# A recurrent kernel on one core: TensorE's program of the GRU stage written out, without a buffer for the current layer's weights

## The reference, cut to what matters

```python
A = (adj != 0).astype(x.dtype)
h = x
for l in range(weight.shape[0]):            # 5 layers
    m = jnp.einsum('bnd,de->bne', h, weight[l])
    agg = jnp.einsum('bij,bid->bjd', A, m)
    h = _gru_cell(agg, h, w_ih, w_hh, b_ih, b_hh)
return h * mask[..., None]
# _gru_cell: gi = agg @ w_ih.T + b_ih; gh = h @ w_hh.T + b_hh
#            r, z = sigmoid(i_r + h_r), sigmoid(i_z + h_z); n = tanh(i_n + r * h_n)
#            h = (1 - z) * n + z * h
```

## Time and profile before

| | |
|---|---|
| median of 3 runs | 584.0 us (583.87 to 584.15) |
| profiled execution, span from first to last instruction | 583.5 us |
| mean granted clock of TensorE over the span | 0.965 |
| TensorE busy | 533.1 us, 91% |
| VectorE busy | 464.4 us, 80% |
| ScalarE busy | 379.3 us, 65% |
| POOL busy | 225.2 us, 39% |
| the 20 copies to wcur, VectorE | 28.5 us |

### The profile page before, as it was taken

How to read it: one execution, slowest core, us unless ns; L and a number is a source line. 1 busy time by engine, 2 the same in 40 slices (tenths; PEclk the granted TensorE clock), 3 DMA queues, 4 the chain that set the end, 5 groups by cost and what they waited for, 6 DMA issues and landing times.

```text
span 583.5 us, 9958 instructions
## 1 busy us (share of the span) xinstructions
PE 533.1 (91%) x2955; PEld 445.0 (76%) x2955; DVE 464.4 (80%) x1000; ACT 379.3 (65%) x703; POOL 225.2 (39%) x278
## 2 busy tenths in 40 slices
PE   5877799999999999999999999999999999999980
PEld 3676689788888888787887887878878878788760
DVE  4416587698888889888888899788888997887884
ACT  3331456667677766687687766877777658667653
POOL 6644351224334242434443323434443333333434
PEclk9676999999999999999999999999999999999995
DMA  4646470000000000000000000000000000000002
GB/s 113 151 105 174 121 203 0 1 0 2 0 0 0 2 0 1 2 18 18 0 18 2 19 0 0 18 18 0 18 0 18 1 1 19 4 14 18 2 18 72
DMA packets 34930, 17.06 MB, mean 29 GB/s; under 512 B 4117, under 2 KB 34810, under 8 KB 34906
## 3 DMA queue, kind: packets, MB, share of 16 engines
q1 hardware_dynamic: 32170, 15.47, 9.9%
q0 software_dynamic: 1280, 0.58, 0.7%
q10 hardware_dynamic: 1456, 0.72, 0.4%
HBM read 12.54 MB, written 4.19 MB: 29 GB/s over the span
## 4 chain that ended last, share of the span: by engine, by line
PE 50%; DVE 16%; SPq 10%; issue 8%; ACT 7%; POOL 7%; DVEq 1%; DMA 0%; ACTq 0%; POOLq 0%
PE p L1036 12%; PE p L1038 12%; PE p L1037 12%; PE p L1029 7%; PE p L1023 5%; DVE wcur L827 5%; SPq L275 4%; SPq L281 3%; POOL rs L417 3%; DVE cg L879 2%; DVE cg L882 2%; ACT rg L605 2%; DVE dg L842 2%; POOL nm L415 2%; SPq L287 2%
## 5 line engine op out<-in xcount | busy, mean ns | idle before, releaser
L458 POOL TENSOR_TENSOR dg<-hT,ng 128x512 f32<-128x512 f32 x80 | 122.3, 1528 | 284.1 <-ACT ng L617 284.1
L1036 PE MATMUL p<-ghi,wcur 128*128 128x512 f32 x240 | 101.4, 422 | 7.6 <-DVE wcur L827 7.6
L1036 PE MATMUL p<-hhi,wh 128*128 128x512 f32 x240 | 101.4, 423 | 4.7 <-ACT zg L615 4.3
L1038 PE MATMUL p<-ghi,wcur 128*128 128x512 f32 x240 | 94.5, 394 | 0.0
L1038 PE MATMUL p<-hhi,wh 128*128 128x512 f32 x240 | 94.4, 393 | 0.0
L1037 PE MATMUL p<-hlo,wh 128*128 128x512 f32 x240 | 94.2, 393 | 0.0
L1037 PE MATMUL p<-glo,wcur 128*128 128x512 f32 x240 | 93.9, 391 | 0.0
L1029 PEld LDWEIGHTS p<-an,nat 128*128 128x128 f32 x640 | 83.4, 191 | 6.3
L879 DVE SCALAR_TENSOR_TENSOR cg<-p,biasc,rg 128x512 f32<-128x512 f32 x80 | 59.8, 748 | 34.6 <-ACT rg L605 34.6
L1029 PE MATMUL p<-an,nat 128*128 128x128 f32 (+1 forms) x640 | 84.2, 274 | 0.0
L605 ACT ACTIVATE rg<-p,gb 128x512 f32<-128x512 f32 x80 | 55.2, 690 | 44.5 <-PE p L1038 39.4
(11 more groups left out here) (125 smaller groups left out, 838.5 us busy)
## 6 DMA issues: line engine op xcount, KB each, us to landing
xn<-in_x_dram SPq DMA_DIRECT2D x8, 512.0 KB, 5.2
an<-in_adj_dram SPq DMA_DIRECT2D x8, 512.0 KB, 7.2
out_dram<-tile_data SPq DMA_DIRECT2D x16, 256.0 KB, 2.3
w<-in_L_gnn_W_dram SPq DMA_DIRECT2D x2, 640.0 KB, 5.2
tile_data<-in_x_dram SPq DMA_DIRECT2D x16, 50.0 KB
tile_data<-in_x_dram POOLq DMA_DIRECT2D x16, 24.0 KB, 2.6
zg<-in_L_gnn_weight_dram ACTq DMA_DIRECT2D x1, 320.0 KB, 3.6
tile_data<-in_x_dram SPq DMA_DIRECT2D x8, 36.0 KB
```

Source lines behind the costliest of these rows:

```text
L458: nc.gpsimd.tensor_tensor(dg[:, w.slot % 2, :], hT[:, w.slot, :], ng[:, w.slot % 2, :], ALU.subtract).then_inc(d_ok, 1)
L1036: MM(bank[:], w[:, 0, cols], xhi, start=start, stop=False)
L1038: return MM(bank[:], w[:, 1, cols], xhi, start=False, stop=stop)
```

## The change

`supergroup` and `windows` get a switch. With it, the layers 1 to 3 are a Python loop, so their windows are written out in the program text, and the layer number is a constant in each. TensorE alone takes the switch. VectorE, ScalarE and POOL keep the hardware loop over layers, and all keep the one over chunks. TensorE reads the fused weights straight from wf. The tile wcur, its semaphore, the 20 copies on VectorE with their waits for z_ps, and TensorE's 20 waits for them are removed.

```diff
-def supergroup(eng, sg, first=False, more=True):
+def supergroup(eng, sg, first=False, more=True, unrolled=False):
...
-    with eng.Fori(1, LAYERS - 1) as l:
-        for slot in range(SLOTS):
-            yield Window(sg, l, slot, "step", "step", **norms(l, slot))
+    if unrolled:
+        for l in range(1, LAYERS - 1):
+            for slot in range(SLOTS):
+                yield Window(sg, l, slot, "step", "step", **norms(l, slot))
+    else:
+        with eng.Fori(1, LAYERS - 1) as l:
+            for slot in range(SLOTS):
+                yield Window(sg, l, slot, "step", "step", **norms(l, slot))
...
-        wcur = sb("wcur", [128, 2, GATES], f32r)
...
-            def layer_weights(l):
-
-                nc.vector.tensor_copy(wcur[:], wf[:, bass.ds(l, 1)].rearrange("p o h e -> p (o h) e")).then_inc(wcur_ok, 1)
-
...
-            layer_weights(0)
...
-                    last_layer = isinstance(w.l, int) and w.l == LAYERS - 1
-                    if s == SLOTS - 1 and not (last_layer and not w.enter):
-
-                        wait_alone(dve, z_ps, k + 1)
-                        layer_weights(0 if last_layer else w.l + 1)
...
-            for w in windows(pe):
+            for w in windows(pe, unrolled=True):
...
-                    if s == 0:
-                        pe.wait_ge(wcur_ok, w.sg * LAYERS + w.l + 1)
...
-                    product(PR, wcur, 0, xhi, xlo, False, True).then_inc(r_ps, 1)
+                    wl_now = wf[:, w.l]
+                    product(PR, wl_now, 0, xhi, xlo, False, True).then_inc(r_ps, 1)
...
-                    product(PI, wcur, 2, xhi, xlo, True, True).then_inc(i_ps, 1)
-                    product(PZ, wcur, 1, xhi, xlo, False, True).then_inc(z_ps, 1)
+                    product(PI, wl_now, 2, xhi, xlo, True, True).then_inc(i_ps, 1)
+                    product(PZ, wl_now, 1, xhi, xlo, False, True).then_inc(z_ps, 1)
```

More of the change, by code:

```diff
@@ L131, in supergroup, with windows @@
                      enter=more and slot >= 2, **share)
-def windows(eng):
+def windows(eng, unrolled=False):
     yield opening(0, first=True)
-    yield from supergroup(eng, 0, first=True)
+    yield from supergroup(eng, 0, first=True, unrolled=unrolled)
     yield opening(1)
     with eng.Fori(1, CHUNKS - 1) as sg:
-        yield from supergroup(eng, sg)
+        yield from supergroup(eng, sg, unrolled=unrolled)
         yield opening(sg + 1)
-    yield from supergroup(eng, CHUNKS - 1, more=False)
+    yield from supergroup(eng, CHUNKS - 1, more=False, unrolled=unrolled)
     yield None
@@ L256, in build @@
         r_ok, z_ok, n_ok, t1_ok, c_ok, d_ok, e_ok, h_ok = map(sem, ("r_ok", "z_ok", "n_ok", "t1_ok", "c_ok", "d_ok", "e_ok", "h_ok"))
-        hi_ok, lo_ok, nat_ok, ghi_ok, glo_ok, wcur_ok = map(sem, (
-            "hi_ok", "lo_ok", "nat_ok", "ghi_ok", "glo_ok", "wcur_ok"))
+        hi_ok, lo_ok, nat_ok, ghi_ok, glo_ok = map(sem, ("hi_ok", "lo_ok", "nat_ok", "ghi_ok", "glo_ok"))
         bn1, ln1_st, ln1_rs, ln1_ok, x2_ok, sum_ok, bn2, ln2_st, ln2_rs, ln2_ok, out_ok = map(sem, (
```

## The result

| | before | after |
|---|---|---|
| median of the runs | 584.08 us (4 runs) | 564.13 us (563.64 to 565.27, 4 runs) |
| span of the profiled execution | 583.5 us | 563.6 us |
| first to last block of neighbour products | 438.50 us | 417.93 us |
| before the first of these blocks | 117.01 us | 117.63 us |
| behind the last | 28.0 us | 28.0 us |

The ratio is 0.9651, interval 0.963 to 0.9672. The forecast was 563.8 us. The profiled execution took 565.27 us, 1.67 above its span. Of the 19.9 us by which the span fell, the stage gave 20.57; the part before it was 0.6 us longer, the tail the same.

A forecast was written before the change was run, and what follows sets the result against it. TensorE was taken to bound the stage, with 22.2 us over its floor. Gains of 11.7 + 7.6 + 0.9 = 20.2 us took the 583.5 us span to 563.3, plus 0.5 gives 563.8 us; range 561.5 to 568.5.

The forecast's parts named there:

- The floor: Recurrent stage: a window with TensorE always busy takes 5.48 us, twelve with new samples 0.44 more; 416.3 us in all.
- Slot 0, 11.7 us: Slot 0 of layers 1 to 4: TensorE no longer waits for the wcur copy, gaining 0.73 us in 16 windows.
- Slot 1, 7.6 us: Slot 1, chunks after the first: without the copy, statistics and zg come earlier, gaining 0.63 us in 12 windows.
- The change of chunk, 0.9 us: Six windows around each chunk change: VectorE gets ahead without the copy; 0.3 us each time, bounds 0 and 2.8 us.
- How 0.48 us of idle time makes 0.73: TensorE after a stop: first product takes 0.50 us in place of 0.39 and its weight load is no longer covered.
- The two bills: The copy costs slot 0 by TensorE's wait, 11.7 us, and slot 1 by delaying statistics and zg, 7.6 us.
- The longer code at nothing: TensorE's code grows from 12 to 20 windows of text per chunk; claimed to cost nothing, covered by queued work.
- rivals 2 and 3: TensorE's longer code: chunk-loop jumps fetch again, 568.4 us, chance 0.06; or TensorE starves for code, 620 us, chance 0.03.
- Rival 2: TensorE's chunk loop: each of two jumps back over 20 windows fetches code, 4.6 us in all, 568.4 us; chance 0.06.
- Rival 1: Slot 1: TensorE's wait moves to zg and stays, so the 7.6 us are not gained, 571.4 us; chance 0.07.
- The port: VectorE and POOL share an SBUF port pair: sixteen copies took 1.64 us, four 0.54, long ones during POOL's subtraction.
- VectorE's busy time: VectorE loses 20 copies and twelve register operations; its busy time was to fall by some 28 us.

The follow-up runs named there:

- the last experiment: Changed kernel with ScalarE's copy of new samples to nat moved ahead of ghi around a chunk change: ratio 0.9603 to the kernel before, median 561.93 us.

## Why the prediction was right, point by point

- *The floor.* 5.48 us was right for every window inside a chunk. For windows with new samples I took 5.48 + 0.44 = 5.92 us, while the row has 5.94; the last experiment shows eight of the twelve at 5.88. The stage at its floor is thus 416.1 and not 416.3 us.
- *Slot 0, 11.7 us.* The sixteen windows fell from a mean of 6.22 to 5.48: 11.8 us.
- *Slot 1, 7.6 us.* Twelve windows fell from 6.11 to 5.48: 7.6 us. The mechanism (statistics, POOL, normalising, zg) is shown from both sides, by the copy moved behind the statistics and by the dummy statistics. The slack was 0.3 us by the forecast. The timeline shows 0.33 up to the product, but the wait stands before the weight load, and a delay of 0.2 us already found the end of the slack.
- *The change of chunk, 0.9 us.* It was 0.43, 0.37 and 0.37, 1.2 us. The guess of 0.3 each was a little low. VectorE's lead did count, in the windows behind, which fell from 6.03, 5.62 and 5.65 to 5.94, 5.47 and 5.47 the first time; the two windows ahead of them kept their ScalarE chain, as supposed.
- *How 0.48 us of idle time makes 0.73.* The numbers were right, the reason given for them was not. In slot 0 the first product behind the transposes takes 0.48 us in the changed kernel too (at 260.09), where nothing stops, so its 0.50 explains almost nothing. The idle time is counted from the modelled end of the four transposes, and without a stop the product begins 0.25 us before that end. The transposes in the kernel before and in the changed one:

```profile
263.96 0.60 PE L1023 MATMUL p<-ident,hT 128*128 128x128 f32 x4
...
259.74 0.60 PE L1016 MATMUL p<-ident,hT 128*128 128x128 f32 x4
```

  The product came 1.08 us after their start before and 0.35 after it now: 0.73 = 0.48 of idle time + 0.25 of lost overlap. At slot 1's stop the parts are 0.36 idle, 0.17 of lost overlap, and 0.11 that the longer first product does add there.
- *The two bills.* The text added them up. They add only when the copy goes: the direct read alone gave 2.1 us, since slot 0's gain is lost again at zg. The forecast was for the whole change, so this did no harm; for a change that took only the wait away, the same sum would have been 11.7 us where 2.1 came.
- *The longer code at nothing.* Right; rivals 2 and 3 fall with the two written-out kernels. Rival 2 also counted two jumps back: a loop of two passes has one, at 328.2 us, and nothing was fetched there. Rival 1 falls with the profile.
- *The port.* Reading the long copies as 0.55 us and a wait of 1.1 for POOL was argued from the trace before; the moved copy shows it.
- *VectorE's busy time.* It fell by 26.3 us, not by some 28. The page counts time once where two records overlap, as the long copy and the statistics behind it do by 0.07 us; that is a part of the difference.
- *The range.* Its lower end, 561.6 us, is said to be all 22.1 us; 584.0 - 22.1 is 561.9.
- *From the span to the median.* I took the 0.5 us between the profiled span and the median of the runs. That held: 564.13 - 563.6 = 0.5. But it is not the time around the span. That is 1.67 us, and the profiled execution of the changed kernel lies 1.1 above its median. And the forecast missed the sum of the stage by 0.4 us (20.57 against 20.2) while the part before it happened to be 0.6 us longer. That the two medians agree within 0.3 us is in part luck; the terms are right by the windows.

## What to carry to other kernels

Cut a pipelined stage into its repeating windows and compare them with the best of their kind: as long as the work in them stays the same, the difference is all that can be gained, and it comes with an address. A copy on an engine that is not the bottleneck can be charged twice, once by who waits for it and once through what is queued behind it; taking away the wait alone may give nothing, as in the layers of three of the four chunks here. Where only an address stands in the way of reading in place, writing the consumer's program out, and only the consumer's, is cheap.

## What the runs showed of the hardware that I had not expected

- A stop of TensorE costs more than the idle time that the trace shows: 0.48 us of idle time lengthened a window by 0.73. Without the stop, the next product began 0.25 us before the modelled end of the work ahead of it, and that overlap is lost too.
- Text of 80 windows, without a branch in the stage, is delivered with no gap on TensorE (417.38 us busy of 417.71). Of the 22 blocks of 16 KB that q8 moved in all, 18 came during the stage. The Trainium skill (Runtime: NRT & Kernel Launch, "Instruction fetch mechanics") calls the crossing of a block mostly hidden; the runs agree. Of its stall for a jump out of the window, no run here shows more than 0.1 us.
- A jump back over the text of 20 windows found all of it still held: no block moved on q8 from 309.7 to 448.4 us, through the whole second pass. What a jump costs that does fetch stays open.
- Whether wf could be read at an address held in a register, inside the loop, was not tried and stays open.
